# Attention block with a ghost-weight FFN: one query tile of each head transposed by VectorE blocks and DMAs instead of TensorE, narrower matmuls, and units in other steps

## The reference

```python
xn = layernorm(x)                                   # x: 1024 x 256
q, k, v = split(xn @ qkv_w + qkv_b)                 # 16 heads of size 128
scores = einsum('hid,hjd->hij', q, k) + alibi_mask  # causal, -slope*(i-j)
ctx = softmax(scores) @ v
attn = ctx @ out_w + out_b
gate, up = xn @ lut[gate_idx].T, xn @ lut[up_idx].T # 688 hidden, 16-entry table
ffn = (silu(gate) * up) @ lut[down_idx].T
return x + attn + ffn
```

## Time and profile before

| | us |
|---|---|
| median of 3 runs | 524.1 (523.46 to 524.34) |
| profiled execution, its own time | 524.43 |
| its span, first to last instruction | 522.6 |
| PE busy | 513.4 (98%) |
| PEld busy | 464.7 (89%) |
| DVE busy | 405.8 (78%) |
| POOL busy | 336.8 (64%) |
| ACT busy | 306.5 (59%) |
| mean granted TensorE clock | 1.000 |

### The profile page before, as it was taken

The page is one execution under the profiler, slowest core; times in us unless marked ns, Lnnn a source line. Parts: engine busy times, 40 slices in busy tenths (PEclk is TensorE's granted clock), DMA queues, the critical chain, the costliest instruction groups (busy, mean ns, idle before and its releaser), DMA issues.

```text
span 522.6 us, 10649 instructions
## 1 busy us (share of the span) xinstructions
PE 513.4 (98%) x3222; PEld 464.7 (89%) x3222; DVE 405.8 (78%) x1064; ACT 306.5 (59%) x657; POOL 336.8 (64%) x388
## 2 busy tenths in 40 slices
PE   8988999999999999999999999999999999999998
PEld 7777889989999889988998999988998899888897
DVE  7689787889778978978788977897897869864451
ACT  4777566656564746666665656474666556564430
POOL 3445867678667966586767866796658647872300
PEclk9999999999999999999999999999999999999999
DMA  7630100010000100000001000010000000000001
GB/s 272 124 81 1 41 22 20 3 36 25 4 16 20 40 0 20 8 33 20 20 0 37 23 2 19 20 40 0 20 0 0 21 1 1 1 2 1 1 21 61
DMA packets 8326, 14.08 MB, mean 27 GB/s; under 512 B 1008, under 2 KB 4080, under 8 KB 8176
## 3 DMA queue, kind: packets, MB, share of 16 engines
q1 hardware_dynamic: 7264, 12.75, 7.8%
q0 software_dynamic: 1040, 1.05, 1.6%
HBM read 12.75 MB, written 1.05 MB: 26 GB/s over the span
## 4 chain that ended last, share of the span: by engine, by line
PE 90%; DMA 3%; DVE 3%; ACT 2%; POOL 1%; issue 1%; DVEq 0%; ACTq 0%; SPq 0%
PE ps_u L400 17%; PE ps_u L402 17%; PE ps_u L401 17%; PE ps_t L519 12%; PE ps_s L402 8%; PE ps_s L401 8%; PE ps_s L400 8%; DMA qk_raw<-w_qk 2%; PE ps_t L402 1%; PE ps_t L401 1%; PE ps_t L400 1%; ACT work L665 1%; ACT p_t_hi L672 1%; DMA acc<-x 1%; DVE work L801 1%
## 5 line engine op out<-in xcount | busy, mean ns | idle before, releaser
L1032 POOL TENSOR_TENSOR w_ffn<-w_ffn,term 128x1088 f32<-128x1088 f32 x60 | 152.5, 2541 | 9.9 <-DVE term L871 9.9
L665 ACT ACTIVATE work<-work,neg_max 128x128 f32<-128x128 f32 (+7 forms) x128 | 98.8, 772 | 30.1 <-DVE neg_max L856 30.1
L672 ACT ACTIVATE p_t_hi<-ps_t 128x512 fp32r<-128x512 f32 (+1 forms) x192 | 86.1, 484 | 35.4 <-PE ps_t L519 34.0
L1010 POOL TENSOR_SCALAR work<-work,inv_sum 128x128 f32<-128x128 f32 (+7 forms) x128 | 106.3, 831 | 0.0
L884 DVE TENSOR_TENSOR p_t_lo<-ps_t,p_t_hi 128x512 fp32r<-128x512 f32 (+1 forms) x192 | 99.1, 544 | 9.2 <-ACT p_t_hi L672 8.6
L856 DVE CUSTOM_DVE_ANT_0 work<-ps_s,alibi 128x128 f32<-128x128 f32 (+7 forms) x128 | 96.1, 751 | 4.1 <-issue 4.1
L519 PE MATMUL ps_t<-ident,work 128*128 128x128 f32 x576 | 84.3, 273 | 3.8 <-POOL work L1010 2.4
L1009 POOL TENSOR_TENSOR pad<-entry 128x1 f32<-128x1 f32 x128 | 27.1, 211 | 92.2 <-DVE inv_sum L878 91.0
L519 PEld LDWEIGHTS ps_t<-ident,work 128*128 128x128 f32 x576 | 68.7, 140 | 11.3 <-POOL work L1010 3.3
L400 PE MATMUL ps_u<-p_t_hi,v_hi 128*128 128x512 f32 x192 | 69.5, 362 | 0.0
L400 PE MATMUL ps_s<-qk_hi 128*128 128x256 f32 (+2 forms) x192 | 67.0, 349 | 0.0
(11 more groups left out here) (125 smaller groups left out, 1161.3 us busy)
## 6 DMA issues: line engine op xcount, KB each, us to landing
qk_raw<-w_qk SPq DMA_DIRECT2D x16, 256.0 KB, 2.6
w_ffn<-idx SPq DMA_DIRECT2D x1, 2176.0 KB, 10.6
v_raw<-w_v SPq DMA_DIRECT2D x8, 256.0 KB, 2.5
o_raw<-w_o SPq DMA_DIRECT2D x8, 256.0 KB, 2.5
acc<-b_out POOLq DMA_DIRECT2D x1, 1024.0 KB, 18.2
out<-acc SPq DMA_DIRECT2D x8, 128.0 KB, 1.7
acc<-x SPq DMA_DIRECT2D x2, 256.0 KB, 3.0
acc<-x SPq DMA_DIRECT2D x1, 512.0 KB, 5.5
```

The lines of the kernel that those rows point to most:

```text
L665: act.activation(slot(i), slot(i), ACT.Exp, bias=neg_max[:, col:col + 1], scale=-1.0, accum_out=row_sum[:, col:col + 1]).then_inc(exp_done, 1)
L672: act.activation(p_rows(0, i, g), ps_t[:, room, 0:len(turned(i, g)) * P].rearrange("p (j q) -> p j q", q=P), ACT.Copy).then_inc(p_hi, 1)
L1010: pool.tensor_scalar(slot(i % NT), slot(i % NT), inv_sum[:, col:col + 1], 1.0, ALU.mult, ALU.mult).then_inc(normed, 1)
L1032: pool.tensor_tensor(piece, piece, term[:, :], ALU.add).then_inc(term_added, 1)
```

## The change

**Tile 4 by another path.** `GROUPS` has no groups for tile 4 (`PLACED`), and PE's `turn` returns at once for it. In its place:

- DVE at step 7 (`turn_blocks`) transposes the 128x640 tile in 32x32 blocks, within its 32 partitions, into a new tensor `blocks`.
- SP (`move`) issues 16 DMAs from SBUF to SBUF, each 32 partitions by 640 bytes, that put block row a, block column b at its transposed place in area 0 of `work`. The moves stand in SP's queue between the refills.
- ACT (`place_hi`) in step 2 of the next head copies the 128x640 result into `p_t_hi`; DVE (`place_lo`) in the same step subtracts into `p_t_lo`. The context of the second half waits for it.

As area 0 of `work` is now busy for longer, tile 0 has an own tensor `work_0`.

**Narrow matmuls.** The scores of tile 0 and the context's last key tile of each half now have 128 columns instead of 256. The zero columns and their memsets go, and `p_t` has a plainer layout.

**Other steps.** The units' table is written anew. Weight conversions stand at steps 6 and 4 instead of 4 and 2, alibi at 2 instead of 3, POOL's additions at 1, 2, 4, 7 instead of 1, 3, 5, 7, and the look-ups at 1, 2, 4, 7 instead of 0, 2, 4, 7 in most heads.

```diff
-QK_W_AT = 4
-V_W_AT = 2
+QK_W_AT = 6
+V_W_AT = 4
 O_W_AT = 6
-ALIBI_AT = 3
-SUM_AT = 1
+ALIBI_AT = 2
+SUM_AT = 1, 2, 4, 7
...
+BLOCKS_AT = 7
+PLACED_HI_AT = 2
+PLACED_LO_AT = 2
+B32 = 32
+BANDS = P // B32
+PLACED = 4
+BAND = (PLACED + 1) * B32
+MOVES = BANDS * BANDS
+GROUPS = [-(-(i + 1) // 4) if i != PLACED else 0 for i in range(NT)]
...
-    return min(max(0, j - 4 * half) * P, 2 * P)
+    return max(0, j - 4 * half) * P
...
     STEADY: [
-        (("q1", 0), ("_out0", 0), ("k1", 1), ("_out1", 1), ("nq0", 2), ("_pv1-", 3), ("_pv1", 4),
-         ("v0", 5), ("v1", 6), ("nk0", 6), ("pv0", 7), ("v2", 7)),
-        (("k1", 0), ("q1", 0), ("v3", 1), ("_out2", 1), ("_out3", 2), ("_pv1-", 4), ("_pv1", 4),
+        (("k1", 0), ("_out0", 0), ("q1", 1), ("nq0", 2), ("_out1", 2), ("_pv1-", 4), ("_pv1", 4),
+         ("v0", 4), ("nk0", 5), ("v1", 5), ("v2", 6), ("pv0", 7)),
+        (("_out2", 0), ("q1", 0), ("k1", 1), ("v3", 2), ("_out3", 2), ("_pv1-", 4), ("_pv1", 4),
          ("nk0", 6), ("nq0", 6), ("pv0", 7)),
     ],
     LAST: [
...
-        (("k1", 0), ("_out2", 0), ("q1", 1), ("_out3", 2), ("v3", 3), ("_pv1-", 5), ("_pv1", 5), ("pv0", 7)),
+        (("q1", 0), ("k1", 0), ("_out2", 2), ("v3", 3), ("_out3", 4), ("_pv1-", 5), ("_pv1", 7),
+         ("pv0", 7)),
...
-TAIL = (("turn", 5), ("gate_up", 0), ("out", 0), ("out", 1), ("turn", 6), ("gate_up", 1), ("turn", 7),
+TAIL = (("turn", 5), ("placed", PLACED), ("gate_up", 0), ("out", 0), ("out", 1), ("turn", 6), ("gate_up", 1), ("turn", 7),
...
+            def move(n, p):
+
+                sp.wait_ge(blocks_turned, head_no(n, p) + 1)
+                for a in range(BANDS):
+                    for b in range(BANDS):
+                        sp.dma_start(work[b * B32:(b + 1) * B32, a * BAND:(a + 1) * BAND],
+                                     blocks[a * B32:(a + 1) * B32, b, :, :].rearrange("p j c -> p (j c)")
+                                     ).then_inc(blocks_moved, 16)
...
                 elif "pv" in name:
                     pe.wait_ge(p_lo, groups_to(n, p, 3 if c == 0 else -1))
+                    if c == 1:
+                        pe.wait_ge(placed_lo, head_no(n, p))
...
-                wide = max(per, 2 * P)
                 for b in range(banks):
-                    last = three(ps_s[:, i % 2, b * HALF:b * HALF + wide],
+                    last = three(ps_s[:, i % 2, b * HALF:b * HALF + per],
...
+                if i == PLACED:
+                    return
                 pe.wait_ge(normed, tile_no(n, p, i - NT if back else i) + 1)
...
+            def place_hi(n, p):
+                act.wait_ge(blocks_moved, head_no(n, p) * (16 * MOVES) + 16 * MOVES)
+                act.activation(placed_rows(0), placed_raw(), ACT.Copy).then_inc(placed_hi, 1)
...
+            def turn_blocks(n, p):
+                dve.wait_ge(normed, tile_no(n, p, PLACED) + 1)
+                if not (isinstance(n, int) and n == 0 and p == 0):
+                    dve.wait_ge(blocks_moved, head_no(n, p) * (16 * MOVES))
+                dve.transpose(blocks[:, :, :, :].rearrange("p b j c -> p j b c"),
+                              slot(PLACED).rearrange("p (j b c) -> p j b c", b=BANDS, c=B32)).then_inc(blocks_turned, 1)
+
+            def place_lo(n, p):
+                dve.wait_ge(placed_hi, head_no(n, p) + 1)
+                dve.tensor_tensor(placed_rows(1), placed_raw(), placed_rows(0).bitcast(F32),
+                                  ALU.subtract).then_inc(placed_lo, 1)
```

More of the change, by code:

```diff
@@ L120 @@
         ("gate_up", 11))
+TERM_FIRST_AT = 4, 5, 6, 7
+TERM_SECOND_AT = 1, 3, 4, 7
+TERM_AT = 1, 2, 4, 7
+TERM_LATE_AT = 1, 3, 5, 7
 def term_at(kind, p, i):
[L125 to L128, removed]
+    if kind == FIRST:
+        at = TERM_SECOND_AT if p else TERM_FIRST_AT
+    else:
+        at = TERM_LATE_AT if (kind, p) == (LAST, 0) else TERM_AT
+    return at.index(i) if i in at else None
 def units_of(kind, p, begun=False):
@@ L252, in turned, with placed_raw, placed_rows, head_no @@
         def turned(i, g):
-            return range(4 * g, min(4 * g + 4, i + 1))
+            return range(4 * g, min(4 * g + 4, i + 1)) if i >= 4 else range(i, -1, -1)
         def p_rows(part, i, g):
[L258 to L265, removed]
+            js, q = turned(i, g), (i % 4) * P
+            if i >= 4:
+                at = pt_at(1, js[0]) + q
+                rows = p_t[part][:, at:at + len(js) * PT_ROW].rearrange("p (j q) -> p j q", q=PT_ROW)
+                return rows[:, :, 0:P]
+            end = pt_at(0, 0) + q + P
+            rows = p_t[part][:, end - len(js) * PT_BACK:end].rearrange("p (j q) -> p j q", q=PT_BACK)
+            return rows[:, :, PT_BACK - P:]
+        def placed_raw():
+            return work[:, 0:BANDS * BAND].rearrange("p (a j c) -> p j a c", a=BANDS, c=B32)
+        def placed_rows(part):
+            rows = p_t[part][:, 0:(PLACED + 1) * PT_ROW].rearrange("p (j q) -> p j q", q=PT_ROW)
+            return rows[:, :, 0:P].rearrange("p j (a c) -> p j a c", c=B32)
+        def head_no(n, p):
+            return 2 * n + p
         def tile_no(n, p, i):
@@ L585, in _ @@
                     gate_up(no)
+                elif what == "placed":
+                    continue
                 elif what == "pv":
                     pe.wait_ge(p_lo, HEADS * HEAD_GROUPS)
+                    pe.wait_ge(placed_lo, HEADS)
                     units += 1
@@ L687, in pair @@
                             p_hi_of(n, p, t, i < LAG)
+                        if i == PLACED_HI_AT and not (kind == FIRST and p == 0):
+                            place_hi(n, p - 1)
                         for name, step in units_of(kind, p):
@@ L743, in _ @@
                     p_hi_of(PAIRS, 0, no, True)
+                elif what == "placed":
+                    place_hi(PAIRS - 1, 1)
                 elif what == "gate_up":
@@ L849, in mask @@
                     dve.wait_ge(alibi_ready, 2 * n + p + 1)
-                if not (kind == FIRST and p == 0 and i < 4):
+                if i == 0 and not (kind == FIRST and p == 0):
+                    dve.wait_ge(p_turned, groups_to(n, p, i - NT))
+                elif i == PLACED and not (kind == FIRST and p == 0):
+                    dve.wait_ge(placed_lo, head_no(n, p))
+                elif i > 4 or i < 4 and not (kind == FIRST and p == 0):
                     dve.wait_ge(p_turned, groups_to(n, p, i - 4))
@@ L904, in pair @@
                             p_lo_of(n, p, t, i < LAG)
+                        if i == PLACED_LO_AT and not (kind == FIRST and p == 0):
+                            place_lo(n, p - 1)
+                        if i == BLOCKS_AT:
+                            turn_blocks(n, p)
                         if i == NT - 1:
@@ L951, in _ @@
                     p_lo_of(PAIRS, 0, no, True)
+                elif what == "placed":
+                    place_lo(PAIRS - 1, 1)
                 elif what == "gate_up":
@@ L1025, in pair @@
                                                ALU.subtract).then_inc(o_w_lo, 1)
-                        if not (kind == FIRST and p == 0) and i % 2 == SUM_AT:
-                            part = i // 2
+                        if not (kind == FIRST and p == 0) and i in SUM_AT:
+                            part = SUM_AT.index(i)
                             pool.wait_ge(term_ready, n * (2 * TERMS) + p * TERMS + part + 1)
```

36 lines of the change are left out of this document (19 added, 17 removed), and 5 rows, old and new, of the table UNITS.

## The result

The changed kernel takes 570.2 us (median of 4 runs, 568.6 to 573.5) against 523.8 for the kernel before, measured beside it: 1.0893 times as long, 95% interval 1.0855 to 1.0932. The forecast was 515.2 with a range of 509 to 525. The changed kernel is 46 us slower than the kernel before.

The account below looks back on a forecast made before the run. The prediction took PE, busy 98% of the span, as the bound. Fewer transposes (-8.7 us), narrow matmuls (-1.7) and the tail (+1.2) summed to -9.2, the rest to 0: from 524.4 to 515.2 us, range 509 to 525.

Parts of the forecast that it names:

- Term 5: SP's 16 moves a head: 9.2 us to issue and land, inside a cover of 10.2 us, so 0 us.
- The third rival: Moves land late in every head from an issue pitch of 0.53 us; at most 18 us, 533; chance 0.04.
- Only shifted: 0: POOL conversions, alibi, look-ups and additions at other steps: same work on engines with room, 0 us.
- Term 1: PE, five transposes fewer in each of 16 heads, 0.108 us each, nothing replacing them: -8.7 us.
- Term 2: PE, 144 matmuls narrowed from 256 to 128 columns, pitch 0.12 falling to 0.108 us: -1.7 us.
- The rival with a quarter of the rate: Narrow float32r matmuls on PE take 0.23 us each, 17.6 us on top: 532.8; chance 0.16.
- Terms 3 and 4: DVE's added transpose and place_lo (0.67 us more a head) stay covered; ACT's work about even: 0 us each.
- Term 6: Tail, no next head to hide the moves: PE waits before turning tile 7, +1.2 us, bounds 0 and +5.
- Term 7: First pair of heads, where PE waits 2.4 us for POOL: taken as 0, bounds -3.6 and +3 us.
- The first rival: Some steps of each head make PE wait 0.1 to 0.5 us: faster by less, 518 to 524; chance 0.16.

Follow-up runs that it names:

- the run of 518.4: Changed kernel with turn_blocks at step 6, POOL's work and the units' table as before (_pv1- at step 4), last placing after turn 7: 518.4 us, ratio 0.9902.

## Why the prediction was wrong

- **Term 5, the moves, is the step that failed.** I took 0.47 us from issue to issue, the largest distance that the trace of before showed, and it is 0.63: 16 x 0.633 = 10.1 us where I had 7.5. I took 9.2 us for the whole and it's 12.0, of which 0.75 is the wait behind the refill; I had put the moves ahead of the weight loads in SP's queue, and they stand behind one. I also gave the moves 10.2 us, read from a kernel in which ACT waited for PE's turn of tile 7 before it; in the changed one ACT is there 8.3 us after the transpose. "They fit by 1 us" became 3.7 us late in the head at 238.28, and 3.4 or more in the heads of the loop: in that head 2.8 us more are needed, and 1.9 us less are given. With the measured cover even the forecast 9.2 us would have been late.
- **The third rival had the mechanism**, with a chance of 0.04. Its point of decision, 0.53 us from issue to issue, was worked out with the cover of 10.2 us; with 8.3 it is (8.3 - 1.7) / 16 = 0.41. That 0.63 lies above both is why it still pointed the right way. The chance was too small for a cover of 1 us that rested on a pitch of other DMAs, one-off loads. Its price was also short: 0.6 us gave 1.1 us a head. Measured with 0.63: 44 us, 2.7 a head. It left out that behind some stops of 2 us the clock falls, and that the units of step 2 are queued behind `place_hi`, so the bank which the context takes is late too.
- **"Only shifted: 0" was wrong for the steps.** The sum has no term at all for the new table of units, which costs 8.4 to 9.5 us. The POOL steps, which it did put at 0, are worth 4 to 10 us one way or the other, depending on what stands beside them (537.0 and 527.1 us with the additions alone moved, 530.8 with all of POOL's work at the old steps). I had checked how busy each engine is, not which operations come to stand in a row. POOL's long operations (2.5 us an addition, 1.3 a weight) before a norm, and a bank whose unit comes just before the context, are what PE waits for in the runs with placing. What the table makes PE wait for without it wasn't followed up.
- **Term 1 was right in the loop**: 1.13 us a pair measured, 1.09 forecast. Over the whole program 4.0 of the 8.7 us arrive (16 x 0.54 is 8.6, to be exact).
- **Term 2 was right in kind and sized at 1.7 for 1.0 to 1.2 us**: the pitch is 0.112, not 0.108, and the interval just reaches 1.7. The rival with a quarter of the rate (0.16) is refuted.
- **Terms 3 and 4** were right: the transpose takes 0.825 us (forecast 0.8), `place_lo` 0.825 (0.82), `place_hi` 0.737 (0.70).
- **Term 6, the tail**: PE waits 4.7 us before turn 7 where I took 1.2, near my bound of 5 and for its reason, the late landing: ACT waits 6.05 us for the last moves.
- **Term 7, the first pair**: PE's 2.4 us of waits for POOL's norm are gone there, but up to 104 us PE waits 4.4 us for `place_lo` and 2.5 for `qk_lo`, the late moves again, where I had bounds of -3.6 and +3.
- **The first rival**, small waits in each step that take back some of the gain, is what the early moves leave with the new table: 527.9, or 526.0 with 8 moves. I had it at 518 to 524.

The sum of terms 1 to 4 was a forecast of a kernel that can be had: 55.3 us a pair was forecast and 55.29 measured in the run of 518.4. That one has early blocks, the old table and POOL's old steps, so it isn't the kernel that was forecast.

## What to carry to other kernels

When work goes from the engine that is full to a chain of small DMAs, count the DMAs times the time of one issue in a row of the same kind, and compare it with the distance between the end of the producer and the first engine that will stand; if the trace has no such row, widen the range of the forecast for it, and don't take a one-off load in its place. Behind the place where an engine can wait, list what it does next, and which buffer (here a PSUM bank) another engine takes next. A table of steps is balanced for one set of waits: change one part at a time, since additions, weights and units each cost or gained 6 to 10 us here, depending on where the others stood.

## What the runs showed that I had not expected

- The cost of an issue: 0.63 us from DMA to DMA in a row of 16 from SBUF to SBUF, the same for 640 or 320 bytes a row and 0.64 for 128 rows of 160 bytes, while a single one takes 0.33 and loads at the start were 0.47 apart.
- `place_lo`, an operation of DVE that reads two SBUF tensors, is held back while an addition of POOL that does so too is under way. With 8 moves `place_lo` falls beside one; in the changed kernel, where it comes late, it doesn't. The timelines of DVE and POOL with 8 moves:

```profile
216.90 1.73 DVE L959 TENSOR_TENSOR p_t_lo<-work,p_t_hi 128x640 fp32r<-128x640 f32 x1
...
215.40 2.54 POOL L1112 TENSOR_TENSOR w_ffn<-w_ffn,term 128x1088 f32<-128x1088 f32 x1 [2.37 <-DVE term L931]
```

DVE's groups by form, with 8 moves (busy us, mean ns, idle before):

```profile
L959 DVE TENSOR_TENSOR p_t_lo<-work,p_t_hi 128x640 fp32r<-128x640 f32 x16 | 27.1, 1694 | 1.6 <-ACT p_t_hi L733 1.6
```

The same group in the changed kernel:

```profile
L959 DVE TENSOR_TENSOR p_t_lo<-work,p_t_hi 128x640 fp32r<-128x640 f32 x16 | 13.2, 825 | 47.8 <-ACT p_t_hi L733 47.8
```

The Trainium skill, "Trainium Architecture — The Big Picture", in its section on what this means for kernel authors, says that DVE and GpSimd share a pair of SBUF ports as an exclusive lock. By that rule `place_lo` would wait for the end of the addition, whenever it starts, and the rows agree: it ends 0.69 us behind the addition here, and 0.69 behind it too in the run with placing at step 3, where it takes 2.23 us (117.13 to 119.36; the addition ends at 118.67). The addition itself takes 2.54 us here, no longer than most. In the run of 518.4 us `place_lo` takes 0.827 us on the mean, so there the two hardly meet.
